# Attentions with heads of 8 in a four-layer kernel: value products in two runs of two key chunks, and the split of the maxima on Pool in the two cross-attentions

## The reference, cut to what matters

```
v = values.reshape(N, v_len, HEADS, HEAD_DIM)          # 16 heads of 8, 512 keys per batch
k = keys.reshape(N, k_len, HEADS, HEAD_DIM)
q = query.reshape(N, q_len, HEADS, HEAD_DIM)           # 256 queries per batch
energy = jnp.einsum('nqhd,nkhd->nhqk', q, k)
attn = jax.nn.softmax(energy / jnp.sqrt(jnp.float32(EMBED_SIZE)), axis=3)
out = jnp.einsum('nhql,nlhd->nqhd', attn, v).reshape(N, q_len, EMBED_SIZE)
return out @ w_out.T + b_out
```

## Time and profile before

| what | value |
|---|---|
| median of 3 runs | 650.02 us (649.97 to 653.85) |
| the profiled execution: its own time | 649.92 us |
| its span in the profile | 648.1 us |
| PE busy | 523.1 us (81%) |
| DVE busy | 401.3 us (62%) |
| ACT busy | 323.6 us (50%) |
| POOL busy | 99.5 us (15%) |
| first cross-attention, first score matmul to last turn of an output | 36.9 to 104.6 us |
| second cross-attention | 213.0 to 281.5 us |

### The profile page before, as it was taken

The page is one execution under the profiler, slowest core; times in us unless marked ns, Lnnn a source line. Parts: engine busy times, 40 slices in busy tenths (PEclk is TensorE's granted clock), DMA queues, the critical chain, the costliest instruction groups (busy, mean ns, idle before and its releaser), DMA issues. The chain is left out here.

```text
span 648.1 us, 9553 instructions
## 1 busy us (share of the span) xinstructions
PE 523.1 (81%) x3481; PEld 309.2 (48%) x3482; DVE 401.3 (62%) x1039; ACT 323.6 (50%) x535; POOL 99.5 (15%) x102
## 2 busy tenths in 40 slices
PE   2669995799984699959788557899999647985997
PEld 2624443477774244435365222455555536553565
DVE  6888853356755988528734465877776366552544
ACT  3626782444432277823635524877777013552421
POOL 4400000000002000000616059500000040000000
PEclk9877999699995779988899777999999966997899
DMA  8900000000000200000000000000000500000000
GB/s 214 407 7 0 2 3 17 0 1 2 0 10 28 98 1 2 1 1 1 0 1 0 1 1 0 0 2 2 1 2 1 196 0 1 1 2 1 1 0 18
DMA packets 3094, 16.55 MB, mean 26 GB/s; under 512 B 348, under 2 KB 860, under 8 KB 2396
## 3 DMA queue, kind: packets, MB, share of 16 engines
q1 hardware_dynamic: 3048, 15.94, 7.2%
HBM read 15.68 MB, written 0.26 MB: 25 GB/s over the span
## 5 line engine op out<-in xcount | busy, mean ns | idle before, releaser
L495 ACT ACTIVATE PR<-ps 128x1024 f32<-128x1024 f32 x80 | 77.1, 982 | 32.0 <-PE ps L1326 16.2
L761 DVE TENSOR_REDUCE mxs<-ps 128x1 f32<-128x512 f32 x128 | 81.5, 682 | 12.6 <-PE ps L1284 11.6
L1270 PE MATMUL ps<-identb,REP 128*96 128x128 bf16 x464 | 39.2, 261 | 30.1 <-DVE REP L298 23.6
L1284 PE MATMUL ps<-Kst,Qst 96*128 96x512 bf16 x128 | 52.3, 458 | 11.2 <-DVE mxs L761 8.8
L843 DVE TENSOR_REDUCE nm<-ps 128x1 f32<-128x512 f32 x64 | 41.2, 685 | 25.5 <-PE ps L1428 25.5
L406 POOL TENSOR_SCALAR ve<-mv 128x4 f32<-128x4 f32 x11 | 2.6, 237 | 350.8 <-DVE mv L716 291.6
L1270 PEld LDWEIGHTS ps<-identb,REP 128*96 128x96 bf16 x464 | 37.6, 158 | 31.8 <-DVE REP L298 19.6
L544 ACT ACTIVATE Qst<-ps,nm 128x512 f32<-128x512 f32 x64 | 44.9, 701 | 4.1 <-DVE nm L843 4.1
L536 ACT COPY PR<-ps 128x512 f32<-128x512 f32 x64 | 37.4, 588 | 18.7 <-PE ps L1439 18.7
L1316 PE MATMUL ps<-Qst,Kst 108*128 108x256 bf16 x256 | 42.7, 293 | 0.5 <-ACT PR L495 0.5
L504 ACT COPY Qst<-ps 12x1024 bf16<-12x1024 bf16 x24 | 24.0, 1000 | 34.8 <-PE ps L1351 34.7
(11 more groups left out here) (320 smaller groups left out, 991.8 us busy)
## 6 DMA issues: line engine op xcount, KB each, us to landing
FC<-in_fc SPq DMA_DIRECT2D x2, 2048.0 KB, 18.5
FC<-in_w SPq DMA_DIRECT2D x1, 2048.0 KB, 8.7
REP<-in_w SPq DMA_DIRECT2D x1, 1536.0 KB, 6.5
FC<-in_w2e SPq DMA_DIRECT2D x1, 1024.0 KB, 10.8
rows_t<-in_rows SPq DMA_DIRECT2D x1, 909.5 KB, 10.9
wd_t<-in_w_d SPq DMA_DIRECT2D x1, 872.5 KB, 24.6
VX<-in_w SPq DMA_DIRECT2D x1, 576.0 KB, 21.6
VX<-in_b SPq DMA_DIRECT2D x1, 576.0 KB, 22.7
```

What stands on the lines that cost most here:

```text
L495: act.activation(PRg[:, g % 2, u * 1024:u * 1024 + width], bank(3 + 2 * (n % 2), 2)[:, 0:width], ACT.Exp, scale=scale).then_inc(s.p_ready, 1)
L761: i = dve.tensor_reduce(m[:, u // 4, u % 4:u % 4 + 1], bank(n % 2), AX_X, ALU.max)
L1270: i = pe.transpose(bankb(lot_bank(n))[0:PAD, h * P:(h + 1) * P], REPv[:, tl % 4, h0 + h, :], identb[:, :])
L1284: i = pe.matmul(bank(n % 2), Qst[0:PAD, h, q0:q0 + P], Kst[0:PAD, h, b * SK:(b + 1) * SK], start=True, stop=True)
```

## The change

Two edits. In both cross-attentions the split of the maxima into three bf16 parts leaves DVE and becomes five Pool instructions for each group, in `split_max`. DVE waits, from step 2 on, for the split of the group whose buffer it is about to overwrite. And PE's value products of a group come in two runs, chunks 0 and 1 in part 1 and chunks 2 and 3 in part 3.

```diff
@@ gpsimd
+            def split_max(a):
+
+                for g in range(G):
+                    m = mxs[:, g % 2, :, :]
+                    to = mp[:, g % 2, :, :, :]
+                    r = mr[:, :].rearrange("p (t h) -> p t h", t=2)
+                    pool.wait_ge(s.smax_read, MAXB[a] + 8 * (g + 1))
+                    if groups(a, g) >= 2:
+                        pool.wait_ge(s.m_turned, groups(a, g) - 1)
+                    link(pool.tensor_scalar(to[:, :, 0, :], m, -1.0, None, ALU.mult))
+                    link(pool.tensor_tensor(r, m, to[:, :, 0, :], ALU.add))
+                    link(pool.tensor_scalar(to[:, :, 1, :], r, -1.0, None, ALU.mult))
+                    link(pool.tensor_tensor(r, r, to[:, :, 1, :], ALU.add))
+                    pool.tensor_scalar(to[:, :, 2, :], r, -1.0, None, ALU.mult).then_inc(s.m_ready, 1)
+                    pool.wait_ge(s.m_ready, groups(a, g) + 1)
...
+            split_max(0)
             rstd_of(1)
             rstd_of(2)
...
                 spread(pool, n)
+            split_max(1)
             rstd_of(4)
@@ vector, attention(a)
                 for step in range(G + 4):
+                    if a < 2 and 2 <= step < G:
+                        dve.wait_ge(s.m_ready, groups(a, step) - 1)
...
-                    if step < G:
+                    if step < G and a == 2:
@@ tensor, attention(a)
-                        if part and 0 <= step - 3 < G:
-                            probs_values(a, step - 3, ([], [0], [1], [2, 3])[part])
+                        if part in (1, 3) and 0 <= step - 3 < G:
+                            probs_values(a, step - 3, [0, 1] if part == 1 else [2, 3])
```

## The result

The changed kernel takes 653.44 us in the median of 22 runs (648.83 to 656.11), the kernel before 650.03 in the same number. The ratio is 1.0046, with a 95% interval of 1.0031 to 1.0062, so 3.0 us slower (2.0 to 4.0); the two medians lie 3.4 us apart. The forecast was 650.4 with a range up to 652.5: the time lies 0.9 us above the range. In a later comparison the ratio was 1.0035 (1.0008 to 1.0062). The one execution that is profiled, 649.52 us, is the second fastest of the 22; it shows where time goes within a step, not what the kernel costs.

A forecast was written before the change was run, and what follows sets the result against it. The prediction took a loop over ACT's work and PE's to bound the middle steps. First-step gains against the moved chunk, clock, periods and tail gave +0.45 us in all, 649.92 to 650.4, range 646.0 to 652.5.

The forecast's parts named there:

- those 0.35 us: Middle steps of the cross-attentions: PE's wait for DVE, put down to the split, would go when Pool takes it.
- the period: Middle step of a cross-attention: 6.83 us forecast against 6.73, so +0.10 in each of steps 4 to 7.
- step 9: End of each cross-attention: ACT's four exponentials held up by the two-chunk run of value products, +0.33 us.
- The loop over ACT: Middle steps: turn of maxima, ACT's copies and exponentials (3.60 us), turn of output, PE's work (3.23 us after) set the period.
- The first steps: Steps 0 to 2 of a cross-attention: taking the split off DVE gains 0.73, 0.31 and 0.79, together 1.83 us.
- The clock: Start of each cross-attention: slow stretch stays 17.05 us, so work brought forward runs slowly; +0.52 us in the first, +0.37 in the second.
- Rival 2: Cross-attention starts: the clock's rise moves with the work, 649.5 us, down to 642 if earlier; chance 0.22, 0.03 for much more.
- Step 8: Step without maxima: no wait for DVE to win back, so the moved chunk costs +0.44 us.
- Pool: Split in the cross-attentions: five linked instructions take 1.8 us, costing nothing up to 4.4 us of cover.
- Rival 3: Turn of the maxima: Pool's split comes too late, at 5.7 us for five instructions giving +18, 668 us; chance 0.04.
- Rival 1: Middle steps: the loop over ACT does not bind and the gain comes through, period 6.3, kernel 644.3 us; chance 0.10.
- Two runs: Value products: one run fewer saves PE about 0.1 us a step, but where PE waits for ACT, so no gain.

The follow-up runs named there:

- e1: Kernel before with only the split moved to Pool, value products still in three runs: 647.17 us, ratio 0.9937 to before.
- e2: Kernel before with only the value products in two runs, the split still on DVE: 655.46 us, ratio 1.0058 to before.
- e8: Changed kernel plus a useless 12 x 1024 copy on ACT behind its copy of the turned maxima: one execution, 662.30 us.
- e3: Changed kernel with the two banks of maxima scores issued apart, around the scores for the exponentials: 648.26 us, ratio 0.9955 to before.
- e6: Changed kernel with each maximum taken over the first 256 of 512 keys: one execution, 641.89 us.
- e4: Kernel before with the two banks of maxima scores issued apart, split still on DVE, three runs: 648.23 us, ratio 0.9948 to before.
- e5: Kernel before with the split on Pool and the banks of maxima scores apart, value products in three runs: 644.20 us, ratio 0.9909 to before.
- e12: e2 measured once more, kernel before with only the two runs of value products: 655.83 us, ratio 1.0091 to before.
- e10: The changed kernel measured once more, nothing altered: 652.81 us, ratio 1.0035 to before.
- e13: The kernel before measured once more, nothing altered: one execution, 648.38 us.
- e11: e1 measured once more, kernel before with only the split moved to Pool: 647.69 us, ratio 0.9968 to before.
- e9: Changed kernel plus a useless 12 x 1024 copy on ACT before its wait for the turned maxima: one execution, 655.25 us.

## Why the prediction was wrong, point by point

- **The failed step** is in the edit that takes the split off DVE: "In a middle step it gives PE those 0.35 us." It gives nothing (e1: 6.76 against 6.73; changed against e2: 7.14 against 7.07). The prediction took the wait of 0.35 us for the split's because the split ended when DVE resumed. It did not ask when the data would have been there anyway: 0.43 us behind the matmul at 70.04, so at 70.47, and DVE resumed at 70.51. The wait is the round trip of two banks issued back to back, and it stayed, at 0.36 us in e1 and 0.31 in the changed kernel.
- **The term it mis-sized** is the period: +0.10 was said, +0.41 measured, in 4 steps of 2 attentions. That is 2.5 us. Put into the sum, with step 9's right size below, it gives 652.5 in place of 650.4, 0.3 and 0.9 under the two medians. That it comes so near is in part luck, since the terms for the clock in the same sum failed.
- **The loop over ACT** was right: 3.59 us in every kernel here but e8 (which lengthens it), 0.44 us more for the moved chunk, 3.60 + 3.23 where the waits for DVE are taken away (e3, e6). I also said that PE would be idle for 0.5 us at `turn_out`; it was not, since part 3's pair waits for DVE in the same way.
- **The first steps** were right. e1 shows edit 1 in them alone. Its second cross-attention and that of before have the fall of the clock at nearly the same place, 4.4 and 4.5 us after the first score matmul. From there to the first turn of the maxima it takes 9.95 us, where it took 10.58; to the second 7.11, where it took 7.40; to the third 5.85, where it took 6.62. That is 0.63, 0.29 and 0.77 us less, where 0.73, 0.31 and 0.79 were said. The kernel before took 6.62 us from the second to the third turn in all four cross-attentions of its two profiles, though 1.0 to 3.5 us of them ran slowly, so PE's clock did not set the pace there. The 0.52 us for the clock no run shows, since no kernel with the split on Pool had the fall and the rise where before had them.
- **The clock**, "so I let the rise keep its distance to it", failed. The slow stretch kept its 17.1 us in 2 of the changed kernel's 4 profiled cross-attentions and was 3.4 and 6.8 us shorter in the other two; with the split on Pool it was shorter in 14 of 16. That is a gain which the sum lacked. Rival 2 had it.
- **Step 8** was right: 5.94 us against 5.51, +0.43. **Step 9** was +0.12, not +0.33: turn of maxima to the next-to-last turn of the output 8.31 us against 8.19 in the second attention.
- **Pool** was right in its price: 1.47 us for the five, 1.8 said, and PE waits for none of it. Rival 3 is out. DVE's new wait for Pool, "hidden by nothing" but put at nothing, cost some 0.06 us a step (last section). Here the Trainium skill's rule (GPSIMD Engine Reference, Engine selection: two-input operations about twice as slow on GpSimd) is not borne out at eight elements: 0.20 us on Pool, 0.17 on DVE.
- **Rival 1**, the gain coming through, was taken as a failure of the loop over ACT. The loop alone would have denied it with both edits (e3: 6.82), and the banks denied it as well. e4 and e5 show that a period of 6.4 can be had, without edit 2 and with the banks apart.
- **Two runs.** The drain at a change of tiling mode, which the Trainium skill's TensorEngine Tiling (Array Packing), Key Properties, tells of, is no guide here to the time: saving one change a step and lengthening the wrong half costs 3.8 us in e2 and 5.9 in e12.

What stays open: the cross-attentions of the two profiles differ by 1.7 us together (135.2 to 136.9), in e10 and e13 by 0.6, while the runs say 3.0 (2.0 to 4.0) and 2.3. Some of the rest lies between the two cross-attentions. From the end of the last turn in the first to the first score matmul of the second it takes 110.2 us in the changed kernel and 108.5 before, 109.6 in e10 and 107.1 in e13. It goes with the slow stretch that follows the first cross-attention: over all 14 profiles the part takes 107.1 to 108.7 us where that stretch is 13.7 us long (before, e13 and six more), 108.8 to 109.6 where it is 17.1 (e10 among them), and 110.2 and 110.1 where it is 20.5 (changed and e11). Whether the edits make it longer or chance does, I have no run that tells.

## What to carry to other kernels

Before an idle time is put down to the work that ended last before it, ask when the data would have come without that work; if at the same moment, removing the work gives nothing. Where a producer has two buffers and fills both back to back, the second cannot be filled again before the first latency and two reads have gone (1.84 us here). Filling them singly between other work took the wait away (e4: 0.33 us a step, a few lines). And in a loop over two engines, a piece of work is free on the side where the other engine binds (e9) and costs nearly in full on its own side (e8), so count it by side, not by its sum.

## What the runs showed of the hardware that I had not expected

- A semaphore wait that has long been satisfied still seems to cost DVE some 0.06 us. In the middle steps DVE, when idle, starts 0.42 to 0.43 us after PE's matmul, whether it was idle for 0.23 us (e2, part 0: 80.47 to 80.89) or for 0.81 (changed, part 2: 69.59 to 70.02). Only at the first bank of a group, and only in the kernels with the split on Pool, it is 0.49 or 0.50 (changed: 73.13 to 73.62). There stands DVE's new wait for the split before last, which had ended 6.2 us earlier (66.94). The delay begins where that wait begins: in the changed kernel's first cross-attention, with the clock slow, it is 0.66 at the first bank of step 1, which has no such wait, and 0.71 at that of step 2. No run takes the wait alone away, so the cause is not proven.
- On Pool an add of 128 x 8 takes 0.20 us, where a power of 128 x 4 takes 1.04.
- PE's slow stretch at the start of a cross-attention lasted 10.2, 13.7 or 17.1 us in 28 cross-attentions, nothing between, and all three of them in the changed kernel (changed, e10) with the same instructions.
- The first score matmul of the first cross-attention lies anywhere from 34.3 to 39.4 us in 14 profiles, though all that precedes it is the same in all kernels. These 5.1 us are more than half of the spread of before's 22 runs (645.8 to 653.9) and more than the change's effect: a single execution says nothing on 3 us.
